# Routing of the first pair moved into the second pair's first two passes, in a two-layer attention and mixture-of-experts kernel

## The reference, cut to what matters

```python
# block 3: slot attention, three iterations over the same context P
Pn = rmsnorm(P, input_norm_w)
k_proj = Pn @ Wk.T;  v_proj = Pn @ Wv.T
for _ in range(3):
    sn = rmsnorm(slots, slot_norm_w)
    q_proj = sn @ Wq.T
    attn = softmax(einsum('bkd,bmd->bkm', q_proj, k_proj) * SCALE, axis=-2)
    attn = attn / (sum(attn, axis=-1, keepdims=True) + EPS)
    updates = einsum('bkm,bmd->bkd', attn, v_proj)
    slots = gru_cell(updates, slots, ...)        # r, z: sigmoid; n: tanh
x = x + tanh(g_xattn[1]) * slots
# block 4: each token is sent to the 2 best of 8 experts
xn = layernorm(x)
probs = softmax(xn @ router_w.T);  topv, topi = top_k(probs, 2)
y = sum over the two experts of  normalised prob * down(silu(gate(xn)) * up(xn))
x = x + tanh(g_ffn[1]) * y
```

## Time and profile before

| | us |
|---|---|
| median of 3 runs | 1300.96 (1299.18 to 1301.58) |
| profiled execution | 1300.48 |
| its span, first to last instruction | 1298.7 |
| TensorE matmul busy | 1114.3 (86%) |
| VectorE busy | 724.2 (56%) |
| ScalarE busy | 383.7 (30%) |
| GpSimd busy | 376.0 (29%) |

### The profile page before, as it was taken

The page is one execution under the profiler, slowest core; times in us unless marked ns, Lnnn a source line. Parts: engine busy times, 40 slices in busy tenths (PEclk is TensorE's granted clock), DMA queues, the critical chain, the costliest instruction groups (busy, mean ns, idle before and its releaser), DMA issues.

```text
span 1298.7 us, 17826 instructions
## 1 busy us (share of the span) xinstructions
PE 1114.3 (86%) x5947; PEld 886.8 (68%) x5947; DVE 724.2 (56%) x1840; ACT 383.7 (30%) x705; POOL 376.0 (29%) x312
## 2 busy tenths in 40 slices
PE   8899899897766657999999967999999649999991
PEld 5467576685556554677887835787878339999990
DVE  5576735757444435465646554445354746666665
ACT  3131221312233224234243333243332123333330
POOL 2423062231435540001111123010101465444710
PEclk9999999999888889999999989999999969999995
DMA  9000051000475734100000000000000586555416
GB/s 327 1 0 34 1 185 28 1 1 5 141 203 161 227 109 137 33 1 1 1 1 1 1 34 34 1 1 1 1 1 1 176 269 186 153 155 168 128 55 210
DMA packets 90851, 102.92 MB, mean 79 GB/s; under 512 B 18336, under 2 KB 75936, under 8 KB 90656
## 3 DMA queue, kind: packets, MB, share of 16 engines
q1 hardware_dynamic: 65920, 59.85, 15.1%
q0 software_dynamic: 20240, 36.72, 9.1%
q10 hardware_dynamic: 4624, 5.51, 1.2%
HBM read 73.31 MB, written 28.74 MB: 79 GB/s over the span
## 4 chain that ended last, share of the span: by engine, by line
PE 50%; issue 18%; DVE 14%; DMA 7%; ACT 4%; POOL 4%; SPq 2%; DVEq 0%; POOLq 0%; ACTq 0%
PE PS L210 12%; PE PS L212 11%; PE PS L211 10%; PE PS L1709 7%; DMA results<-y,place_of 3%; PE PS L1597 2%; POOL routed L843 2%; PE PS L1569 2%; PE PS L1481 1%; PE PS L1681 1%; DMA split<-down_w 1%; POOL rstd L836 1%; DMA places<-routed 1%; PE PS L1475 1%; DVE hs L588 1%
## 5 line engine op out<-in xcount | busy, mean ns | idle before, releaser
L836 POOL TENSOR_TENSOR rstd<-ve,minus_half 128x4 f32<-128x4 f32 x40 | 41.3, 1033 | 350.9 <-DVE ve L1101 210.9
L535 POOL DMA_INDIRECT results<-y,place_of x80 | 78.2, 978 | 184.2 <-DVE y L624 110.5
L1481 PE MATMUL PS<-ones_bf 128*128 128x512 bf16 x393 | 103.7, 410 | 19.1 <-DMA routed<-S,dest 16.0
L210 PE MATMUL PS<-xt,split 128*128 128x256 f32 x312 | 90.2, 289 | 9.2 <-issue 6.1
L211 PE MATMUL PS<-xt,split 128*128 128x256 f32 x312 | 89.0, 285 | 0.0
L212 PE MATMUL PS<-xt,split 128*128 128x256 f32 x312 | 88.9, 285 | 0.0
L1709 PE MATMUL PS<-VP,HB 128*128 128x257 f32 x384 | 85.8, 382 | 0.7 <-DVE VP L1407 0.5
L843 POOL DMA_INDIRECT routed<-S,dest x64 | 66.1, 1033 | 67.1 <-DVE dest L1181 49.3
L1481 PEld LDWEIGHTS PS<-ones_bf 128*128 128x128 bf16 x393 | 39.0, 105 | 66.7 <-issue 34.2
L210 PE MATMUL PS<-split,hs 128*128 128x256 f32 x184 | 59.7, 324 | 25.8 <-DVE hs L588 19.9
L1709 PEld LDWEIGHTS PS<-VP,HB 128*128 128x128 f32 x384 | 72.5, 190 | 13.5 <-DVE VP L1407 3.4
(11 more groups left out here) (338 smaller groups left out, 2955.0 us busy)
## 6 DMA issues: line engine op xcount, KB each, us to landing
xg<-routed SPq DMA_DIRECT2D x42, 256.0 KB
HB<-results SPq DMA_DIRECT2D x16, 512.0 KB, 5.6
routed<-blank SPq DMA_DIRECT2D x20, 264.0 KB
raw<-gate_w SPq DMA_DIRECT2D x8, 512.0 KB
raw<-up_w SPq DMA_DIRECT2D x8, 512.0 KB
raw<-down_w SPq DMA_DIRECT2D x8, 512.0 KB
split<-m_w POOLq DMA_DIRECT2D x12, 256.0 KB, 3.2
split<-gate_w POOLq DMA_DIRECT2D x6, 512.0 KB
```

The source lines that it names most:

```text
L210: pe.matmul(out_, a[1], b[0], start=first, stop=False)
L535: pool.indirect_dma_start(out=results[m], out_offset=bass.IndirectOffsetOnAxis(ap=place_of[:, a:a + 1], axis=0), in_=w.y[:, a], in_offset= ...
L836: pool.tensor_tensor(rstd[h][:], ve[h][:], minus_half[:], ALU.pow).then_inc(sem(name), 1)
L1481: pe.matmul(free.rearrange("p (a b) -> p a b", b=P), ones_bf[:], ones_bf[:].unsqueeze(1).to_broadcast([P, TT, P]), start=True, stop=True)
```

## The change

`ORDER_C` gets two more strings for TensorE, ScalarE and VectorE (five in all): `between` the pairs, and `begin` for the first pass of the second pair, whose items with `<` belong to the pair before. In other passes a number ahead of `<` names the pass in which the item runs (`1<scatter0`).

```diff
     "pe": ("ctxT0 ctxT1 kk0 kk1 slotT0 slotT1 ss0 rsb0",
            "scoreA0 ss1 scoreB0 rsb1 upd0 scoreA1 uT0 scoreB1 ha0 ra0 na0 za0 upd1 hb0 rb0 uT1 nb0 zb0 "
-           "ha1 ra1 na1 +ss0 za1 !final0 hb1 +rsb0 rb1 nb1 zb1 !xnT0",
-           "logits0 lt0 final1 rank0 >slotT0 >ctxT0 >kk0 xnT1 logits1 lt1 rank1 >slotT1 >ctxT1 >kk1 >ss0 >rsb0",
+           "ha1 ra1 na1 +ss0 !final0 za1 hb1 +rsb0 rb1 nb1 !xnT0 zb1",
+           "logits0 >ctxT0 lt0 final1 >slotT0 >kk0 >ss0 >rsb0 xnT1",
+           "scoreA0 <logits1 scoreB0 <lt1 ctxT1 slotT1 upd0 kk1 ss1 uT0 rsb1 ha0 ra0 scoreA1 na0 scoreB1 za0 hb0 upd1 rb0 nb0 uT1 zb0 "
+           "ha1 ra1 na1 +ss0 <rank0 za1 <rank1 hb1 +rsb0 rb1 nb1 zb1",
     "act": ...
-           "ha1 +sq0 ra1 na1 za1 hb1 +sn0 rb1 nb1 zb1 +sq1 +hi0 +hi1 !xnT0",
-           "lt0 exp0 >slotT0 >ctxT0 >kk0 xnT1 >sq0 lt1 exp1 >slotT1 >ctxT1 >kk1 >sq1 >sn0",
+           "ha1 +sq0 ra1 na1 za1 hb1 +sn0 rb1 nb1 !xnT0 zb1 +sq1 +hi0 +hi1",
+           "lt0 >ctxT0 >slotT0 >sq0 >kk0 exp0 >sn0 xnT1",
+           "expA0 <lt1 expB0 ctxT1 slotT1 sq1 kk1 <exp1 uT0 sn1 ha0 ra0 expA1 na0 expB1 za0 hb0 rb0 nb0 uT1 zb0 "
+           "ha1 +sq0 ra1 na1 za1 hb1 +sn0 rb1 nb1 zb1 +sq1 +hi0 +hi1",
     "dve": ...
-           "ga0 za0 1:slots0 2:slots1 upd1 gb0 uT1 zb0 ga1 +ve0 za1 !stats0 !final0 +sn0 +snlo0 gb1 zb1 +lo0 +lo1 !xnT0",
-           "choose0 place0 >slotT0 >ctxT0 stats1 final1 >kk0 xnT1 choose1 place1 >slotT1 >ctxT1 >ve0 >kk1 >sn0 >snlo0",
+           "ga0 za0 1:slots0 2:slots1 upd1 gb0 uT1 zb0 ga1 +ve0 !stats0 za1 !final0 +sn0 +snlo0 gb1 !xnT0 zb1 +lo0 +lo1",
+           "chooseA0 >ctxT0 stats1 >slotT0 >ve0 final1 >kk0 >sn0 >snlo0 xnT1",
+           "maxA0 maxB0 <chooseA1 vp0 ctxT1 slotT1 upd0 kk1 ve1 uT0 sn1 snlo1 ga0 maxA1 maxB1 vp1 <chooseB0 za0 upd1 gb0 uT1 zb0 "
+           "<chooseB1 ga1 +ve0 <place0 za1 <place1 +sn0 +snlo0 gb1 zb1 +lo0 +lo1",
     "pool": ...
-             "ve1 1:ctx0 2:ctx1 ha0 1:slots0 2:slots1 hb0 +ve0 ha1 !final0 hb1",
-             "scatter0 final1 scatter1 >ve0",
+             "ve1 1<scatter0 1<scatter1 1:ctx0 2:ctx1 ha0 1:slots0 2:slots1 hb0 +ve0 ha1 !final0 hb1",
+             "final1 >ve0",
+             "ve1 ha0 hb0 +ve0 ha1 hb1",
@@
+                elif "<" in stage:
+                    when, stage = stage.split("<")
+                    pair, it = (pair - 1, ITERS - 1) if pair and it == int(when or 0) else (PAIRS, 0)
@@
-                    for item in each.split():
+                    for item in (begin if pair and it == 0 else each).split():
                         yield from one(item, pair, it)
-                for item in behind[pair].split():
+                for item in (between if pair < PAIRS - 1 else behind).split():
```

`choose` is cut in two: `choose_begin` (maximum and difference, up to what the `exp` needs) and the rest. So that both pairs' work fits beside each other, data move to other places, and waits with them:

```diff
+        def token_logits(m, h):
+            return bank(h, 1 + 2 * m)[:, 2 * TT * E:3 * TT * E]
+        def token_ranks(m, n, h):
+            return bank(0, n)[:, 0:TT * E] if m == 1 and n < 2 else bank(h, 1 + 2 * m)[:, 0:TT * E]
+        def squares(h):
+            return S1[h][:].rearrange("p (c a) d -> p c (a d)", c=C)
+        def updates(n, h):
+            return S2[h] if n < 2 else SN[h]
@@ ScalarE
+                    if n >= 2:
+                        act.wait_ge(sem(f"slot_new{h}"), slot_count(n - 2, ITERS))
@@
-                    if it == 0:
-                        act.wait_ge(sem("kk_lo"), n + 1)
-                    act.activation(S0[h][:], HT[h][:], ACT.Square).then_inc(sem("slot_sq"), 1)
+                    act.activation(squares(h), HT[h][:], ACT.Square).then_inc(sem("slot_sq"), 1)
@@ VectorE: the sums are read from bank 2 (before 0), the root from bank 3 (before 1)
+                    if it == 0:
+                        dve.wait_ge(sem("kk_lo"), n + 1)
@@ the wait for the first pair's scatters moves from upd (first pass) to final
-                    if n >= 2 and it == 0:
-                        dve.wait_ge(sem(f"scattered{h}"), 16 * 2 * TT * (PAIRS + 1))
+                    if n >= 2:
+                        dve.wait_ge(sem(f"scattered{h}"), 16 * 2 * TT * (PAIRS + 1))
@@ TensorE
-                        pe.wait_ge(sem("xnT_lo"), B + n - 1)       # slotT
+                        pe.wait_ge(sem("rt_sub"), B + n - 1)
-                        pe.wait_ge(sem("dest"), B + n - 1)         # ctxT
+                        pe.wait_ge(sem("logits_out"), B + n - 1)
-                    elif n == 2:                                   # kk
-                        spin(bank(1, 2), 11)
-                    elif n == 3:
-                        pe.wait_ge(sem("slot_lo0"), split_count(2, 0))
-                        spin(bank(0, 2), 11)
-                    if h == 1:                                     # ss
-                        spin(idle_bank(n, q - 1), 2)
+                    if h == 1 and it:
+                        pe.wait_ge(sem("hn_out"), C * (q - 1))
+                        spin(bank(1, 0), 2)
+                    if it == 0:
+                        pe.wait_ge(sem(f"slot_lo{h}"), split_count(n, 0))
-                    if h == 1:                                     # rsb
-                        spin(bank(1, 2), 2)
-                    elif it == 0:
-                        pe.wait_ge(sem("slot_lo0"), split_count(n, 0))
-                        spin(bank(0, 2), 6)
+                    if h == 1 and it:
+                        spin(bank(1, 0), 2)
+                    elif q == 0:
+                        pe.wait_ge(sem("kk_lo"), 1)
+                        spin(bank(0, 0), 6)
+                    if h == 0 and n >= 2 and it == 1:              # scoreA, scoreB
+                        pe.wait_ge(sem("dest"), B + PAIRS)
-                    if h == 0:                                     # upd
+                    if h == 0 and not (n >= 2 and it == 0):
                         spin(bank(1, 2), 8)
-                    spin(bank(h, 0), (10, 6, 4, 4)[n])             # logits
+                    spin(bank(h, 0), (0, 0, 4, 4)[n])
-                    spin(bank(h, 0), (10, 13, 10, 14)[n])          # rank
+                    if n >= 2:
+                        spin(bank(h, 0), (10, 14)[h])
```

More of the change, by code:

```diff
@@ L324, in stages_c @@
         def stages_c(engine):
-            before, each, *behind = ORDER_C[engine]
+            before, each, between, begin, behind = ORDER_C[engine]
             def one(item, pair, it):
@@ L1117, in lo_part, with choose_begin @@
                 dve.tensor_tensor(RT[h][:, 1], ps, RT[h][:, 0].bitcast(F32), ALU.subtract).then_inc(sem(name), 1)
-            def choose(m, n, h, eps, gate):
+            def choose_begin(m, n, h):
                 R = RTM[h]
-                lg = bank(h, 1)[:, 2 * TT * E:3 * TT * E].rearrange("p (j e) -> p j e", e=E)
+                lg = token_logits(m, h).rearrange("p (j e) -> p j e", e=E)
                 q = m * B + n
@@ L1127, in choose @@
                 dve.tensor_tensor(R[:, 0], lg, R[:, 7, :, 0:1].to_broadcast([P, TT, E]), ALU.subtract).then_inc(sem("rt_sub"), 1)
+            def choose(m, n, h, eps, gate):
+                R = RTM[h]
+                q = m * B + n
                 dve.wait_ge(sem("rt_exp"), q + 1)
@@ L1172, in place @@
                 dve.wait_ge(sem("rank_ps"), q + 1)
[L1173 removed]
+                rank = token_ranks(m, n, h).rearrange("p (j e) -> p j e", e=E)
                 step(dve.tensor_tensor(R[:, 0], rank, ebase[:].unsqueeze(1).to_broadcast([P, TT, E]), ALU.add))
@@ L1417, in _ @@
                     for j in range(TT):
-                        ins = dve.tensor_scalar(S2[h][:, j], bank(h, j)[:, 0:D], SM[h][:, 4, j:j + 1], None, ALU.mult)
+                        ins = dve.tensor_scalar(updates(n, h)[:, j], bank(h, j)[:, 0:D], SM[h][:, 4, j:j + 1], None, ALU.mult)
                     ins.then_inc(sem("upd"), 1)
@@ L1454, in _ @@
                     turned_lo(1, n, h)
-                elif stage == "choose":
+                elif stage == "chooseA":
+                    choose_begin(1, n, h)
+                elif stage == "chooseB":
                     choose(1, n, h, 1e-9, 3)
@@ L1506, in ranks @@
                 pe.wait_ge(sem("chosen"), m * B + n + 1)
-                pe.matmul(bank(h, 1)[:, 0:TT * E], tri[:], rbf[h][:, 0].rearrange("p j e -> p (j e)"), start=True, stop=False)
-                pe.matmul(bank(h, 1)[:, 0:TT * E], ones_bf[:], rbf[h][:, 1].rearrange("p j e -> p (j e)"), start=False, stop=True)\
+                pe.matmul(token_ranks(m, n, h), tri[:], rbf[h][:, 0].rearrange("p j e -> p (j e)"), start=True, stop=False)
+                pe.matmul(token_ranks(m, n, h), ones_bf[:], rbf[h][:, 1].rearrange("p j e -> p (j e)"), start=False, stop=True)\
                   .then_inc(sem("rank_ps"), 1)
-            def idle_bank(n, q):
-                pe.wait_ge(sem("slot_lo1"), split_count(n, 0))
-                if q:
-                    pe.wait_ge(sem("r_out"), C * q)
-                return bank(1, 2)
             pe.wait_ge(sem("pool_c"), 11)
@@ L1712, in _ @@
                     pe.wait_ge(sem("upd"), q + 1)
```

(2 more changed lines are left out.)

12 lines of the change are left out of this document (6 added, 6 removed), and 2 rows, old and new, of the table ORDER_C.

## The result

The changed kernel took 1283.16 us (median of four runs, 1273.17 to 1292.08), the kernel before 1300.60 (four runs, 1299.18 to 1301.58): ratio 0.987, interval 0.9832 to 0.9907. It is faster, by 17.4 us; I had said 28.7, and 1283 lies just above my range of 1266 to 1282. The runs of the kernel before lie within 2.4 us, those of the changed one spread over 18.9: something in it costs more in some executions than in others.

The account below looks back on a forecast made before the run. No single engine bounds the span; between the pairs TensorE mostly waits, some 59 us. Terms -37.3 + 7.3 + 0.3 - 0.5 - 0.2 + 1.7 = -28.7 take 1300.48 to 1271.8, stated as 1272 us, range 1266 to 1282.

Parts of the forecast that it names:

- (c): Second pair's second pass, GpSimd: the 16 scatters take 21 us where 29 are free, cost 0; bounds 0 to 33.
- rival 4: Slow scatters in the second pass delay the gates' subtractions: slower than before, 1303 to 1306 us; chance 0.02 in full.
- (f): TensorE's clock between the pairs, fillers gone: one short stretch at half speed, +1.7 us; ends 0 and 3.5.
- (a): Stretch up to the second pair's first score: score starts at 765.3 us, for 802.66 before, -37.3 us.
- (b): Second pair's first pass, bound by TensorE, gets the work taken out between pairs: 69.1 to 76.4 us, +7.3.
- Rival 2: First pass gives back more, by doubled waits (5 us) or falling clock (1.7 to 3.5): 1277 to 1281 us; chance 0.22.
- (d): End of the second pair: the split of lane 0's rows now stands before the last state, -0.5 us.
- (e): First pair's start: sum of squares waits for the slots' low part, +0.2; four fillers gone, -0.4; together -0.2 us.
- theory A: From the experiments: 16 scatters in an unbroken row beside busy TensorE make its signals late, from about the tenth on.

Follow-up runs that it names:

- the profile without the stall: Changed kernel, unaltered, run again: profiled execution 1274.87 us, second pass 70.6 us, without TensorE's wait (8.03 us in the profile after) and the slow matmuls behind it.
- the two kernels of eight and eight: Changed kernel with lane 0's eight scatters in the second pass, lane 1's in the third: 1268.65 us, ratio 0.9788; with TensorE fillers too: 1266.21 us, 0.9773.
- the second or fourth chip: Chips of two experiment groups, no late signals in five profiles; kernel before took 1296.14 and 1295.49 us there.
- the first or third: Chips of the two other experiment groups, late signals in every profile; kernel before 1300.18 and 1302.44 us, changed kernel unaltered 1279.04 and 1280.68 us.

## Why the prediction was wrong, point by point

- **(c) is the step that failed.** "16 in all ... 29 us free: 0", with the sentence that nothing waits for the scatters but the expert stage. I priced them as time on GpSimd's queue only, and that price was right: 20.3 us of 29, steady, and 21.0 in the profile without the stall, with 5.91 us left ahead of the subtraction. What I had no term for is that scatters in flight can hold back another engine's signals. Cost: 81.3 to 81.6 us for the second pass in the four profiles with the stall there, 70.6 in the one without, so some 11 us in an execution that has it. With the scatters in the third pass the loss moved there (84.2 for 74.1), on the same chip: that it comes from the scatters is shown. My rival 4 named them, but by slowness of each: none was slow in the profile after, one of 16 took 1.82 us in that without the stall. The rows that I had picked from before show no row longer than eight beside the passes. But its trace has the 16 in a row ahead of the first expert stage, and behind them VectorE's wait of 6.86 us by "remote" at 344.69: the warning was there, and I did not look at it.
- **(f) was mis-sized.** I had 1.7 us; fillers take 3.0 out of the handover and 1.5 out of the first pass. After the waits of 1.63, 1.25 and 1.58 us the root product took 2.08 us and six fillers 2.77, where the earlier trace rows had 1.16 and ten in 2.32. A single wait of 1.84 us ahead of 748.92 in before had left the matmul behind it at 0.40 us; here it is several waits close to each other, with light work between. The Trainium skill (TensorE: Matmul & The Clock Gate, HAM oscillation) says that idle gaps throttle the array again; the 0.63 us matmuls behind the wait of 8.03 us agree. The second place, the root of lane 1 at 798.81, I had as a wait (2.4 us, measured 2.32) without the half clock behind it.
- **(a) was right.** 20.2 us from router product to score; 20.15 measured with the clock held, 22.7 to 23.1 without. The product itself came 212.7 us after the first pair's first score (216.91 before), 0.4 less than I had.
- **(b) was right.** 76.4 us; 76.46 with the clock held, 78.0 without, 79.4 in the profile after. Rival 2's first half, longer waits, did not happen; its second, the clock, did, with 1.5 to 3 us.
- **(d)**: -0.5 predicted; third pass and what follows to the expert stage -0.95 in the profile after, -1.3 in the two kernels of eight and eight (118.96 before, 117.70 and 117.63).
- **(e)**: this profile shows +5.9, with the clock low ahead of the first pair (its sum of squares took 3.41 us, 1.84 before). It is hardly the change: on one chip the unaltered start of the kernel before had the first score at 533.96, and three kernels with the changed start had it at 531.13 to 534.42. It is a large part of the 8.9 us by which this execution lies over its own median.
- **The sum.** Where signals are late, the execution without the stall took 1274.87 us beside a median of 1300.18 before, -25.3. Where none is late, the kernel with its scatters in two passes took 1268.65 for 1296.14, -27.5. I had said -28.7. The mechanisms of the handover were all there; the miss is (c), and a smaller part (f).

**Open.** What holds the signals back, and why it does so on some chips only. The recording of the profile may have a part in it, as the traces with late signals are also those without landing times. The sixteenth scatter's data of the profile after, issued at 881.97, are in by 884.2, about as soon as those of the eight of the second chip, 2.4 us after their issue each: so it is not a backlog of their bytes, as the expectations of theory A called it. Open too is what the changed kernel takes on the second or fourth chip, and the one of eight and eight on the first or third: one run of each would part the chip from the length of the row. Only this shape of scatter was run.

## What to carry to other kernels

An instruction that is hidden on its own queue is not yet free: before DMAs are moved beside a busy engine, look in the trace at what like DMAs do to that engine's signals where they stand now. Lateness is seen as idle time that ends by "remote" though the producer is long done. When experiments run on several chips, let one kernel run on all of them, or find a part that all kernels share and compare it first: here it was the chip, and not only the edit, that differed between the kernels with the loss and those without. And when the runs of a changed kernel spread far more than those before, profile more than one: the difference between a fast and a slow execution names the stretch. Where fillers go, look at the length of a matmul behind each wait: after the waits of 1.25 to 1.63 us here it was nearly doubled, after one of 1.84 us in before it was not.

## What the hardware showed that I had not expected

- Signals of finished matmuls came up to 8.6 us behind the matmuls' recorded ends while 16 indirect scatters of 1.27 us each went out in a row, in all seven profiles with 16 beside a pass, the first of them between the tenth and the twelfth scatter; ahead of the first expert stage in three profiles one was 1.5 us late behind the sixth; with 12 in a row it was up to 3.6 us.
- It depends on the chip or the session: the 16 in a row ahead of the first expert stage did it in nine of nine profiles on some, in none of five on two others. Rows of eight beside a pass were run only on those two.
- The changed kernel took 1273 to 1292 us in 15 runs, those with rows of eight, on the two other chips, 1261 to 1275 in 25.
- At the second pair's end one scatter is slow in every kernel (3.19 to 4.26 us in fourteen profiles), as in the earlier trace rows; here in after, where VectorE's subtraction of two SBUF operands ran from 1038.40:

```profile
1039.14 3.44 POOL L869 DMA_INDIRECT routed<-S,dest  x1 [0.30 <-issue]
```
